# Zeroing only the rows behind each expert's last row, in a fused mLSTM, FFN and mixture-of-experts kernel

## The reference, cut to what matters

```python
x = x + mlstm(ln(x), ctx, ctx)             # 8 heads of 32, decaying causal weights
x = x + bitlinear_ffn(ln(x))               # 256 -> 1024 -> 256, ternary weights
x = x + linear_attention(ln(x), ctx, ctx)
# mixture of experts: 8 experts, 2 for each token
p = softmax(ln(x) @ Wg + bg); w, idx = top_k(p, 2); w = w / sum(w)
x = x + sum over the 2 experts of w * (gelu(ln(x) @ W1[e] + b1[e]) @ W2[e] + b2[e])
```

## Time and profile before

| what | value |
|---|---|
| median of 3 runs | 720.91 us (720.3 to 721.1) |
| profiled execution, its own time | 720.72 us |
| its span, first to last instruction | 718.9 us |
| PE busy | 476.2 us (66%) |
| DVE busy | 443.0 us (62%) |
| POOL busy | 358.5 us (50%) |
| ACT busy | 253.4 us (35%) |
| HBM read, written | 38.54 MB, 28.48 MB |

### The profile page before, as it was taken

The page is one execution under the profiler, slowest core; times in us unless marked ns, Lnnn a source line. Parts: engine busy times, 40 slices in busy tenths (PEclk is TensorE's granted clock), DMA queues, the critical chain, the costliest instruction groups (busy, mean ns, idle before and its releaser), DMA issues. The chain is left out here.

```text
span 718.9 us, 13417 instructions
## 1 busy us (share of the span) xinstructions
PE 476.2 (66%) x4288; PEld 352.2 (49%) x4288; DVE 443.0 (62%) x1134; ACT 253.4 (35%) x656; POOL 358.5 (50%) x428
## 2 busy tenths in 40 slices
PE   2979999500455555542555653169999999999940
PEld 2747777400122222221444543167888788878820
DVE  4234787775788898975667676435455445545427
ACT  0335555200433333334553521034334434443400
POOL 4347788538256666666322656613433443444320
PEclk9999999755555555555775675579999999999975
DMA  7919688840011111111000111231111111111019
GB/s 243 161 59 304 227 289 275 285 155 0 1 58 58 58 58 58 58 59 47 29 16 29 45 45 59 89 119 39 48 59 46 47 53 55 47 46 40 30 51 329
DMA packets 55309, 67.81 MB, mean 94 GB/s; under 512 B 21744, under 2 KB 38256, under 8 KB 55120
## 3 DMA queue, kind: packets, MB, share of 16 engines
q1 hardware_dynamic: 48048, 53.31, 24.0%
q0 software_dynamic: 3408, 9.34, 3.7%
q10 hardware_dynamic: 3792, 4.38, 1.8%
HBM read 38.54 MB, written 28.48 MB: 93 GB/s over the span
## 5 line engine op out<-in xcount | busy, mean ns | idle before, releaser
L1536 ACT ACTIVATE region<-ehp,aux 128x128 f32<-128x128 f32 x312 | 88.9, 368 | 117.6 <-PE ehp L1479 117.6
L1551 POOL CAST vaug<-region 128x512 bf16<-128x512 f32 x78 | 47.9, 614 | 133.7 <-ACT region L1536 133.7
L1479 PE MATMUL ehp<-aux,w1hi 128*128 128x128 bf16 x1248 | 110.8, 221 | 0.5 <-DVE aux L1581 0.5
L1479 PE MATMUL ehp<-aux,w1lo 128*128 128x128 bf16 x624 | 108.4, 221 | 0.0
L1492 PE MATMUL eyp<-w2pair,vaug 128*128 x312 | 105.3, 379 | 0.0
L1479 PEld LDWEIGHTS ehp<-aux,w1hi 128*128 x1248 | 98.7, 99 | 5.5 <-DVE aux L1581 0.7
L1495 PE MATMUL eyp<-w2pair,vaug 128*128 x312 | 78.7, 273 | 0.0
L1595 DVE TENSOR_TENSOR aux<-eyp,wstage 128x256 f32<-128x256 f32 x39 | 16.6, 425 | 74.1 <-PE eyp L1492 74.1
L1479 PEld LDWEIGHTS ehp<-aux,w1lo 128*128 x624 | 61.7, 99 | 0.0
L1588 DVE TENSOR_TENSOR vaug<-region,vaug 128x512 bf16<-128x512 f32 x78 | 50.2, 684 | 1.0 <-POOL vaug L1551 1.0
L591 ACT ACTIVATE w2pair<-argp,w2pair 128x128 f32<-128x128 f32 x128 | 36.4, 367 | 37.9 <-PE argp L525 37.9
(11 more groups left out here) (268 smaller groups left out, 1121.6 us busy)
## 6 DMA issues: line engine op xcount, KB each, us to landing
wstage<-in_wall SPq DMA_DIRECT2D x64, 256.0 KB, 2.7
row_buf<-aux SPq DMA_DIRECT2D x5, 1935.0 KB, 9.2
row_buf<-aux SPq DMA_DIRECT2D x3, 2322.0 KB, 9.9
aux<-row_buf SPq DMA_DIRECT2D x39, 129.0 KB, 2.1
x_all<-in_x SPq DMA_DIRECT2D x4, 512.0 KB, 8.7
w2pair<-in_ctxT ACTq DMA_DIRECT2D x2, 1024.0 KB, 11.4
vaug<-in_ctx SPq DMA_DIRECT2D x16, 128.0 KB, 4.0
aux<-in_ctxT SPq DMA_DIRECT2D x8, 256.0 KB, 2.7
```

The source lines that it names most:

```text
L1479: last = pe.matmul(hp[:, j % 2, f, :], w1(cc * NF + f, part), xT[:, j % 2, cc, xpart, :], start=(cc == 0 and n == 0), stop=(cc == NC - 1 a ...
L1536: last = act.activation(hf[:, j % 2, f * BLK:(f + 1) * BLK], hp[:, j % 2, f, :], ACT.Gelu, bias=b1T[:, bass.ds(e * NF + f, 1)])
L1551: pool.tensor_copy(hhi[:, j % 3, n], hf[:, j % 2, n]).then_inc(hi_done, 1)
```

## The change

The 8 large DMAs of zeros in the mLSTM stage go, with the wait for them there and before the first scatter. Each expert now has 2048 + 128 rows (`RS`) in `row_buf`. In the routing stage POOL clears a small tile `zeros` (128 by 516 bf16); SyncE clears the 128 spare rows with it behind its last load; and once the counts are there, VectorE makes one more small addition, `zero_at`, the row behind each expert's last one, after which SyncE and ScalarE each write 128 rows of zeros for 4 of the 8 experts (`clear_tails`). SyncE ends the block with a wait for all 9 of these DMAs. Apart from that, `kp` has 8 buffers instead of 2, and `weighted(b)` waits for nothing and stands earlier in POOL's order.

```diff
-            kp = space.cut(P, 2, D)
+            kp = space.cut(P, B, D)
...
-                        z = slice(cuts[b], cuts[b + 1])
-                        sp.dma_start(flat_rows[:, z, :], zeros.bitcast(BF16).unsqueeze(1).broadcast_to(
-                            [P, cuts[b + 1] - cuts[b], ZROWS * PW])).then_inc(zero_in, 16)
-                    sp.wait_ge(zero_in, 16 * B)
...
                     def weighted(b):
-                        if b >= 2:
-                            pool.wait_ge(st_ready, b - 1)
-                        pool.tensor_tensor(kp[:, b % 2].rearrange("p (h c) -> p h c", h=NH),
+                        pool.tensor_tensor(kp[:, b].rearrange("p (h c) -> p h c", h=NH),
...
                             split_piece(pool, b, p)
-                            if p == 1 and b + 2 < B:
-                                weighted(b + 2)
+                            if p % 2 and 2 * b + 2 + p // 2 < B:
+                                weighted(2 * b + 2 + p // 2)
                             if p == 2 and b >= 2:
                                 residual(b - 2)
...
+            def clear_tails(eng, experts):
+
+                eng.wait_ge(end_ready, 2)
+                for e in experts:
+                    at = eng.value_load(zero_at[0:1, e:e + 1], min_val=e * RS, max_val=e * RS + T)
+                    eng.dma_start(row_buf[bass.ds(at, BLK), :], zeros).then_inc(zero_in, 16)
...
+                    sp.wait_ge(made, 1)
+                    sp.dma_start(row_buf[E * RS:E * RS + BLK, :], zeros).then_inc(zero_in, 16)
                     sp.wait_ge(small_in, 48)
+                    clear_tails(sp, range(0, E, 2))
+                    sp.wait_ge(zero_in, 16 * (E + 1))
...
-                        if b == 0:
-                            pool.wait_ge(zero_in, 16 * B)
...
                     pool.memset(oneb, 1.0)
+                    pool.memset(zeros, 0.0).then_inc(made, 1)
...
-                    act.wait_ge(gap_ready, 1)
+                    act.wait_ge(end_ready, 1)
                     act.activation(e2, gap, ACT.Exp).then_inc(ex_ready, 1)
+                    clear_tails(act, range(1, E, 2))
...
-                    dve.tensor_tensor(gap, m2, m1, ALU.subtract).then_inc(gap_ready, 1)
+                    dve.tensor_tensor(gap, m2, m1, ALU.subtract).then_inc(end_ready, 1)
                     dve.wait_ge(tot_ready, 1)
+                    dve.tensor_tensor(zero_at, rk[:, 0:E], first_row, ALU.add).then_inc(end_ready, 1)
```

More of the change, by code:

```diff
@@ L43 @@
 MASKED = -30000.0
-ZROWS = 3
+RS = T + BLK
 META = 2
@@ L150, in program @@
         w2pair = sb("w2pair", [P, 2 * E * NF * D], BF16)
-        aux_t = sb("aux", [P, 4864])
+        aux_t = sb("aux", [P, 5120])
         wstage = sb("wstage", [P, NC * FE])
@@ L166, in program @@
         region, aux, vaug_flat = region_t[:, :], aux_t[:, :], vaug_t[:, :]
-        row_buf = nc.dram_tensor("row_buf", [E * T + BLK, PW], BF16, kind="Internal").ap()
+        row_buf = nc.dram_tensor("row_buf", [E * RS + BLK, PW], BF16, kind="Internal").ap()
         y_buf = nc.dram_tensor("y_buf", [NBLK * BLK + 2 * T, D], F32, kind="Internal").ap()
@@ L226, in program @@
         gain = space.cut(P, D)
-        zeros = space.cut(P, ZROWS * PW // 2, pool=1)
         after_gates = space.pools[0][1]
@@ L287, in _ @@
                     pool.memset(ones_s, 1.0)
-                    pool.memset(zeros, 0.0)
                     for q in range(2):
@@ L482, in _ @@
                 def _(sp):
-                    flat_rows = row_buf.rearrange("(p k) n -> p (k n)", p=P).rearrange("p (k n) -> p k n", n=ZROWS * PW)
-                    nz = flat_rows.shape[1]
-                    cuts = [nz * z // B for z in range(B + 1)]
                     for b in range(B):
@@ L500, in state @@
                         for g in range(NC):
-                            last = pe.matmul(argp[:, 0, g * VG:(g + 1) * VG], kp[:, b % 2, g * P:(g + 1) * P],
+                            last = pe.matmul(argp[:, 0, g * VG:(g + 1) * VG], kp[:, b, g * P:(g + 1) * P],
                                              vaug[:, TB * b, g * VG:(g + 1) * VG], start=True, stop=True)
@@ L959, in program @@
                 sem("l_ready"), sem("lg_read"))
-            c_ready, rank_ready, slot_ready, tot_ready, gap_ready, ex_ready = (
-                sem("c_ready"), sem("rank_ready"), sem("slot_ready"), sem("tot_ready"), sem("gap_ready"), sem("ex_ready"))
+            c_ready, rank_ready, slot_ready, tot_ready, end_ready, ex_ready = (
+                sem("c_ready"), sem("rank_ready"), sem("slot_ready"), sem("tot_ready"), sem("end_ready"), sem("ex_ready"))
             NPK = 4
@@ L978, in program @@
             xT = space.cut(P, NC, S)
+            zeros = space.cut(P, PW, dt=BF16)
+            zero_at = space.cut(P, E, dt=I32)
             packed = space.cut(P, NPK, TB, PW // 2)
@@ L1076, in _ @@
                     pool.iota(low, pattern=[[-1, E]], base=E, channel_multiplier=0, allow_small_or_imprecise_dtypes=True)
-                    pool.iota(first_row, pattern=[[T, E]], base=0, channel_multiplier=0, allow_small_or_imprecise_dtypes=True)
+                    pool.iota(first_row, pattern=[[RS, E]], base=0, channel_multiplier=0, allow_small_or_imprecise_dtypes=True)
                     pool.iota(meta[:, 0], pattern=[[P, NT]], base=NBLK * BLK, channel_multiplier=1, allow_small_or_imprecise_dtypes=True)
@@ L1209, in _ @@
                             if j == min(chosen_in):
-                                pe.wait_ge(made, 1)
+                                pe.wait_ge(made, 2)
                             rank(chosen_in[j])
@@ L1312, in choose @@
                         if g == 0:
-                            dve.wait_ge(made, 1)
+                            dve.wait_ge(made, 2)
                         dve.wait_ge(l_ready, last_batch[g] + 1)
@@ L1378, in _ @@
                     chain(dve.tensor_scalar(st, st, float(BLK), None, ALU.mult))
-                    chain(dve.scalar_tensor_tensor(st, be, float(T), st, ALU.mult, ALU.add))
-                    chain(dve.tensor_scalar(row_at, st, float(E * T), None, ALU.min))
+                    chain(dve.scalar_tensor_tensor(st, be, float(RS), st, ALU.mult, ALU.add))
+                    chain(dve.tensor_scalar(row_at, st, float(E * RS), None, ALU.min))
                     dve.wait_ge(ex_ready, 1)
@@ L1419, in load @@
                             sp.wait_ge(at_ready, j - NX + 1)
-                        at = sp.value_load(row_at[0:1, j:j + 1], min_val=0, max_val=E * T)
+                        at = sp.value_load(row_at[0:1, j:j + 1], min_val=0, max_val=E * RS)
                         sp.dma_start(xg[:, j % NX], row_buf[bass.ds(at, BLK), :]).then_inc(x_in[j % NX], 16)
```

## The result

The changed kernel takes 722.83 us in the median of 7 runs (720.27 to 723.35), the kernel before 720.78 beside it (7 runs, 720.08 to 721.66). The ratio is 1.0026, with a 95% interval of 1.0014 to 1.0039. The forecast was 722.8. The profiled execution took 722.04 us, with a span of 720.2 (before: 720.72 and 718.9).

A forecast was written before the change was run, and what follows sets the result against it. TensorE was taken to bound the mLSTM stage and VectorE to end the routing block. Terms 0 + 0.34 + 0.2 + 1.42 = +1.96 on 720.72 gave 722.7, or 722.9 on the median; forecast 722.8, range 720.7 to 724.6.

The forecast's parts named there:

- SyncE so ends the block at 469.19 instead of 467.77: +1.42: End of routing stage: SyncE's wait for the tails outlasts VectorE, adding 1.42 us; +1.12 or +2.52 with other landings.
- 0.92 + 3 × 1.17 + 2.4 = 6.83 us: Routing stage's end: VectorE's addition and first address load, three more load-and-DMA pairs at 1.17, then 2.4 us landing.
- the rival of the long landing: Routing stage's end: the tails land in 4.5 us instead of 2.4, +2.1 more, 724.9 us; chance 0.10.
- The estimate of 2.3 us: Landing of a tail's write by the Trainium skill, in place of 2.4 us; the sum would be 0.1 less.
- VectorE therefore ends this block: Routing stage's end: VectorE's last instruction ends at 467.77, so any wait ending later delays everything behind it.
- The rival "faster": Before the counts in routing: VectorE's stall is lost, up to 4.17 us gained, 718.6 us; chance 0.12.
- Zeros out of the mLSTM stage: 0: mLSTM stage: removing the zeros gains 0; POOL's 4.08 us wait for weights becomes a longer wait for VectorE.
- The mLSTM stage changes by a microsecond or more: Sign against the forecast, which had the mLSTM stage 100.6 us long within 0.5.
- The idle time before the counts is not 4.7 us: Sign against the forecast: VectorE's idle time before the counts, at the routing stage's end, differs from 4.7 us.
- `weighted` early, +0.34: mLSTM stage: the new order makes the three batches to 117.35 take 33.97 us against 33.63, +0.34.
- The small tile in the routing stage, +0.2: Start of routing: POOL's memset may stretch VectorE's first centring by 0 to 0.7 us, taken as 0.2.

The follow-up runs named there:

- fixed tails: Changed kernel with old zeros kept and all eight tails written to fixed rows without waiting for the counts, against the kernel before: 724.16 us, ratio 1.0013.
- the changed kernel's second profile: Changed kernel run again, unchanged, in the first follow-up series, against the kernel before: 725.65 us, ratio 1.0043.
- The tails alone: Changed kernel with `kp` and the weighted keys as before, against the kernel before: 725.44 us (6 runs), ratio 1.0042.
- both edits: Count matmuls right behind the last ranks, scatters' landing wait moved to SyncE; against the kernel before: 0.9994 in the kernel before, 1.0027 in the changed one.
- the wait on SyncE: Changed kernel with the wait for the scatters' landing moved from POOL's end to SyncE's, against the kernel before: 723.44 us, ratio 1.0024.
- the counts edit: TensorE's 16 count matmuls right behind the last ranks, no second turn; against the kernel before: 0.9971 in the kernel before, 1.0024 in the changed one.

## Why the prediction was right, and where it was not

**The forecast's mechanism is shown, with a term mis-sized.** "SyncE so ends the block at 469.19 instead of 467.77: +1.42" holds as a mechanism: alone, the tails have the whole cost (1.0042), and in their profiles fixed tails, or half as many, end before VectorE. The size is 2.1 to 2.6 us between VectorE's end and SyncE's, not 1.42. From the counts taken to SyncE's wait met, the sum was 0.92 + 3 × 1.17 + 2.4 = 6.83 us. In the changed kernel's second profile it is 467.51 − 466.28 = 1.23 to the first issue, 3.35 for three more, and 3.2 for the landing of the last: 7.8. The pair was right (1.12 for 1.17); the first issue comes 0.3 later, and the landing is 0.8 longer than the 2.4 taken from POOL's single scatters, within the bounds of 2.1 and 3.5. The six profiles with late counts and eight tails agree on the sum (7.5 to 8.1) but not on its terms. The tails alone and the changed kernel with both edits have it as above (last landings of 3.5 and 3.3). With the old zeros beside the tails, with the wait on SyncE and with the counts edit the first issue comes 2.78, 2.78 and 2.11 us behind the counts, the three more take 2.6 to 3.2, and the last landing 2.2 to 2.6. So no single term was too small in all of them, and the rival of the long landing had the right sign in three of six. The number in flight does not explain the landing: eight writes have medians of 3.1, 3.1, 2.6, 2.4, 2.4 and 2.2, four have 2.4.
The Trainium skill (DMA: Bandwidth & Descriptors, "Latency and other measured facts") says that the fixed cost of a DMA is mostly the access to HBM, 0.2 us on average and 2 us at high load. No run here shows what load the memory had, so none can show this. The estimate of 2.3 us that the prediction takes from the same page, whose fit is of DMAs issued by GpSimd, lies within the medians of 2.2 to 3.1 us of these six profiles; the sum goes by the landing of the last write, 2.2 to 3.5.

**"VectorE therefore ends this block" was wrong by a tie.** POOL was done 0.1 us behind it. I had priced the end of the block by the first fetch of rows, 1.50 us behind VectorE, without asking who else arrives. The forecast did not suffer, since SyncE's new wait ends behind both.

**The rival "faster" was mispriced for that reason.** Its condition came true in the very profile of after, and the forecast of 718.6 did not: POOL's landing (3.7 us for 1.6, its scatters now sharing the DMA engines with eight tails) and its drain of 2.69 us ended the block 14.2 us behind the counts. In the profile that I predicted from, the same luck could gain 0.1 us at most; where the stall is 6.9 us, as in that of `kp` alone, it could gain 2.2. That the tails' traffic made the scatters late here is argued from this one profile: with the tails issued earlier, and with them later, POOL's wait had its old length.

**The idle time before the counts** belongs to an execution, not to a program: 0.61 and 6.96 us in the same one, 4.7 to 7.7 in thirteen of fourteen. The profile of before wasn't the worst place to stand, but to price anything on its 4.74 was luck.

**"Zeros out of the mLSTM stage: 0" is right.** Batches with a DMA share of 0.3 are not shorter than those with 0.9, and the kernel with both old zeros and tails is not slower than the variants without the zeros. "The mLSTM stage changes by a microsecond or more" was to refute me, and it did change, by 1.45 us. The unchanged kernel does the same when its clock falls later, so the test was badly chosen: it took one execution's stage as the kernel's. "The idle time before the counts is not 4.7 us" was badly chosen for the same reason.

**`weighted` early, +0.34:** +0.26 in the first pair of profiles. From the first product of the stage to the last, 84.0 us (83.8 to 84.2) in the five profiles with the old order and 84.2 (83.9 to 84.4) in the nine with the new one. The ranges overlap, and the kernel with this edit alone has 83.9 there and a ratio of 1.0010, which no run here tells from 1. A cost of 0.1 to 0.2 us is the difference of the means, not shown. In the first profile the pattern is the one foreseen: the late instruction of VectorE takes 1.02 us in the two batches that had been spared (before, 0.18 us at 94.59, and 0.17 at 105.63).

```profile
93.86 1.02 DVE L668 SCALAR_TENSOR_TENSOR w2pair<-w2pair 128x16 f32<-128x16 f32 x1
...
105.11 1.02 DVE L668 SCALAR_TENSOR_TENSOR w2pair<-w2pair 128x16 f32<-128x16 f32 x1
...
116.39 1.02 DVE L668 SCALAR_TENSOR_TENSOR w2pair<-w2pair 128x16 f32<-128x16 f32 x1
```

**The small tile in the routing stage, +0.2:** the memset takes 0.53 us and the time from the block's start to the last ranks is the same with it and without it, within a scatter of up to 2 us between executions. The term was too high or zero.

**The sum.** +2.4 for the tails, 0.1 to 0.2 for `weighted`, 0 for the rest: 2.5 to 2.6 us, or 1.0035. Measured were 1.0026, 1.0043 and, with both edits on either side, 2.5 us; with the old zeros beside the tails only 1.0008, with the counts edit on either side 3.6 us. The forecast of +1.96 erred by one microsecond in its main term (1.42 for 2.4), and the two small terms, which were too high, gave some of it back. That 722.8 was met within 0.03 us is luck: one program under two names differs by 0.9 us, and the profile beside it got its time in other stages.

**What stays open.** Why the counts come late. It is neither the zeros, nor the tails, nor `kp`, and in the four profiles without TensorE's second turn they are late as well; TensorE's own drain ends with the wait, within 0.7 us, in all of them, so the time seems to lie on its side. What the profiles don't show is what it waits for. Also open: the combination stage took 21.7 us in the first profile of after and 21.4 in that of its counts edit, 20.0 to 20.9 in all others. And the medians of the kernel with old zeros and tails (1.0008) and of that with fixed tails (1.0013), which do not separate what their profiles do.

## What to carry to other kernels

At the end of a block ask every queue when it is done, not only the engine that you watch: a wait and then a drain of 2.7 us can stand level with it, and this decides both what a delay costs and what a lost stall would bring. Bytes that are hidden are worth nothing; a chain of few small DMAs behind the last number that is known is paid as far as it outlasts the other work that waits for that number, here 7.5 to 8.1 us of loads, issues and one landing against 5.6 us of VectorE. And take a stage's length from several executions before an unexplained microsecond of one profile enters a sum or a test.

## What the hardware showed

- POOL drains for 2.69 us at the end of the routing block, behind the landing of its own scatters, in every profile with that wait on POOL (3.23 us at the end of the expert stage). Without the wait ahead of it the drain took 7.9 us, but ended 2.9 us behind the last scatter's issue instead of 4.5.
- Writes of 129 KB into DRAM land after 2.4 us in the median of four, and after 2.2 to 3.1 in the medians of eight in six profiles. In the one profile where POOL went on scattering while they went out, the median is 4.0 and the longest 5.5.
- An address load and a DMA by it follow one another every 1.12 us on SyncE in the changed kernel's second profile, 0.87 in that with the old zeros, 1.29 in the first.
- At the end of the routing stage VectorE waits 0.7 us for the last ranks and 0.6 for the counts, or 2.3 to 2.6 and then 4.7 to 7.7 us, by the execution.
- The fall of TensorE's clock at the end of the mLSTM stage comes before or behind its last 16 matmuls (3.2 to 3.6 or 2.02 us for them), and moves the stage's end by 1.4 us, in one and the same program.
